# Shorter filler matmuls in the attention steps of an eight-core attention and expert layer

## What is computed

```python
h = _layernorm(x) * (1 + ca) + sa
x = x + ga * attn(h)
h = _layernorm(x) * (1 + cb) + sb
x = x + gb * ffn(h)

def attn(x):                       # 8 x 2048 x 1024, 16 heads of 64
    Q, K, V = x @ wq + bq, x @ wk + bk, x @ wv + bv
    Q, K, V = (a.reshape(B * H, S, D) for a in (Q, K, V))
    attn = softmax(einsum('bqd,bkd->bqk', Q, K) / sqrt(D))
    ctx = einsum('bqk,bkd->bqd', attn, V).reshape(B, S, E)
    return _layernorm(ctx @ wo + bo + x)

def ffn(x):                        # 8 experts, a gate for each token
    weights = softmax(x @ gate_w + gate_b), those below 0.1 dropped, rescaled
    return sum(weights[:, e] * (x @ expert_w[e] + expert_b[e]) for e in range(8))
```

## Time and profile before

| | |
|---|---|
| median of 2 runs | 2497.0 us (2492.66 to 2501.34) |
| the profiled execution | 2490.43 us |
| its span, slowest core (7) | 2488.9 us; the cores from 2454.0 to 2488.9 |
| mean granted clock, core 7 | 0.841 (the cores from 0.839 to 0.847) |
| TensorE busy | 1823.1 us, 73% of the span |
| VectorE busy | 903.3 us, 36% |
| ScalarE busy | 720.5 us, 29% |

### The profile page before, as it was taken

How to read it: one execution, slowest core, us unless ns; L and a number is a source line. 1 busy time by engine, 2 the same in 40 slices (tenths; PEclk the granted TensorE clock), 3 DMA queues, 4 the chain that set the end, 5 groups by cost and what they waited for, 6 DMA issues and landing times.

```text
span 2488.9 us, 23765 instructions; the slowest of 8 cores (2454.0 to 2488.9 us)
## 1 busy us (share of the span) xinstructions
PE 1823.1 (73%) x7658; PEld 719.0 (29%) x7658; DVE 903.3 (36%) x1481; ACT 720.5 (29%) x692; POOL 42.6 (2%) x78
## 2 busy tenths in 40 slices
PE   0122069978958968877886995896888299999993
PEld 0000032232223224223223322422422134444441
DVE  1443050062163144335316215324432643333336
ACT  0000007607604622740660561373274000000000
POOL 0000000000000000000000000000000000000000
PEclk9855578889869879987897986997898589999997
DMA  8642940040022022013002102202200121232103
GB/s 224 192 125 41 221 152 1 1 148 1 1 73 76 1 72 77 1 53 97 1 28 83 39 1 72 76 1 72 77 1 5 21 47 34 35 54 48 34 1 135
DMA packets 41837, 150.48 MB, mean 60 GB/s; under 512 B 15597, under 2 KB 15597, under 8 KB 37112
## 3 DMA queue, kind: packets, MB, share of 16 engines
q0 software_dynamic: 20480, 96.51, 14.7%
q1 hardware_dynamic: 21240, 52.46, 6.9%
HBM read 151.09 MB, written 16.78 MB: 67 GB/s over the span
## 4 chain that ended last, share of the span: by engine, by line
PE 56%; DVE 11%; ACT 8%; issue 5%; DMA 4%; DVEq 2%; ACTq 1%; POOLq 0%; SPq 0%
PE pbA L1083 9%; PE pbB L1083 9%; PE pbC L868 9%; PE pbD L914 6%; PE pbA L895 5%; ACT hT L906 5%; PE pbB L895 5%; DMA wbuf<-wbh 3%; PE pbA L771 3%; PE pbD L920 2%; PE pbD L616 2%; PE pbD L743 2%; DVEq L54 2%; DVE recipB L951 2%; ACT recipB L936 1%
## 5 line engine op out<-in xcount | busy, mean ns | idle before, releaser
L906 ACT ACTIVATE hT<-pbA,cm,c 128x1024 bf16<-128x1024 f32 x256 | 308.6, 1206 | 477.0 <-PE pbA L895 473.0
L868 PE MATMUL pbC<-hT,Vbuf 128*65 128x512 bf16 x1024 | 336.4, 413 | 40.8 <-ACT hT L906 38.1
L906 ACT ACTIVATE hT<-pbB,cm,c 128x1024 bf16<-128x1024 f32 x256 | 308.7, 1206 | 96.8 <-PE pbB L895 91.5
L951 DVE CAST recipB<-pbD 64x1024 bf16<-64x1024 f32 x32 | 38.9, 1217 | 797.7 <-PE pbD L946 797.7
L1083 PE MATMUL pbA<-We,h2T 128*128 128x512 bf16 x1024 | 232.8, 381 | 1.8 <-DVE facc L1056 1.8
L1083 PE MATMUL pbB<-We,h2T 128*128 128x512 bf16 x1024 | 231.5, 379 | 0.0
L914 PE MATMUL pbD<-CAb 128*128 128x512 bf16 x512 | 213.9, 418 | 22.4 <-DVE recipB L951 22.4
L895 PE MATMUL pbA<-Qasm,Kasm 64*128 64x512 bf16 x512 | 167.3, 409 | 1.1 <-DMA Kasm<-Kasm 1.1
L895 PE MATMUL pbB<-Qasm,Kasm 64*128 64x512 bf16 x512 | 166.3, 407 | 0.0
L771 PE MATMUL pbA<-hT,wbuf 128*128 128x256 bf16 x1024 | 145.1, 293 | 20.6 <-DVE Qasm L786 7.1
L920 PE MATMUL pbD<-CAb 128*128 128x256 bf16 x512 | 149.0, 291 | 0.0
(11 more groups left out here) (165 smaller groups left out, 1461.2 us busy)
## 6 DMA issues: line engine op xcount, KB each, us to landing
wbuf<-wbh POOLq DMA_DIRECT2D x32, 2048.0 KB, 9.4
wmstage<-wmod SPq DMA_DIRECT2D x32, 768.0 KB, 5.0
We<-ew POOLq DMA_DIRECT2D x8, 2048.0 KB, 14.5
xsb<-x SPq DMA_DIRECT2D x16, 512.0 KB, 14.4
wbh<-wbuf SPq DMA_DIRECT2D x4, 2048.0 KB, 12.9
out<-xsb SPq DMA_DIRECT2D x16, 512.0 KB, 2.7
wbuf<-wq POOLq DMA_DIRECT2D x1, 2048.0 KB, 18.6
wbuf<-wk POOLq DMA_DIRECT2D x1, 2048.0 KB, 38.4
```

What stands on the lines that cost most here:

```text
L868: P.emit("tensor", lambda e, h01=h01, gp=gp, q4=q4, par=par: e.matmul(psc[:, 512 * q4:512 * (q4 + 1)], vview[:, h01, gp, 0:65], PT[:, 1024 ...
L906: P.emit("scalar", lambda e, par=par: e.activation(PT[:, 1024 * par:1024 * (par + 1)], pss[par][:, :], AF.Exp, bias=cm3[:, :], scale=c0125 ...
L951: P.emit("vector", lambda e: e.tensor_copy(recipB[0:64, :], psr[:, :]), waits=[("t2", tv)], writes=("recipB",), inc="v1")
```

## The change

In every attention step the first filler shrinks from 512 columns to 128, and the second filler, 256 columns behind the context, goes. The increment of semaphore `m1` at step 15 moves to the filler that stays.

```diff
                     P.emit("tensor", lambda e: e.matmul(
-                        pbD[:, 0:512], CAb[:, 0:128], CAb[:, 0:512],
-                        start=True, stop=True), waits=fw)
+                        pbD[:, 0:128], CAb[:, 0:128], CAb[:, 0:128],
+                        start=True, stop=True), waits=fw,
+                        inc=("m1" if gp == 15 else None))
                     if pend is not None:
                         emit_mm2(*pend)
                     pend = (k, seg)
-                    P.emit("tensor", lambda e: e.matmul(
-                        pbD[:, 0:256], CAb[:, 0:128], CAb[:, 0:256],
-                        start=True, stop=True),
-                        inc=("m1" if gp == 15 else None))
```

## The result

| | before | changed |
|---|---|---|
| median | 2493.9 us (10 runs) | 2677.6 us (11 runs, lowest 2661.6) |
| ratio | 1 | 1.0716, 95% interval 1.0686 to 1.0747 |
| span of the slowest core, profiled | 2488.9 us | 2666.2 us (core 0) |
| mean granted clock of that core | 0.841 | 0.711 |
| first segments of octets 1 to 7 at full clock, all cores | 55 of 56 | 47 of 56 |

Some executions of a program on eight cores run with one die's clock held lower whatever the kernel; they are in the medians of this text but in none of its ratios or profiles, and where they leave only one or two others (runs 8, 9 and 12), the times of these stand in place of a median and a ratio.

What follows compares the result with a forecast made beforehand. The prediction took TensorE to pace the attention steps, with the granted clock deciding. Its terms (+151 later segments, +29 boundaries, +8 and -8 first segments, -23 luck) sum to +157, about 2647, stated as 2650 us, range 2550 to 2730.

Steps and rivals of the forecast that it cites:

- 24 later segments, luck included: Attention segments after each octet's first: 32.7 us each at half clock against 26.4, +151 us, before savings from lucky ones.
- their boundaries: Stretches between segments' exponentials, 4.5 us before: reached at half clock, each takes +1.2 us, times 24, +29 us.
- eight first segments: First segment of each octet: octet 0's stays at half clock, +8 us; seven at full clock save 1.2 us each, -8.
- outside attention: Projections, out-projection and experts: nothing moves, as they wait on transfers or run dense.
- The 23 us of luck: Later segments on core 7: 2 of 24 keep full clock, each 11.7 us better than a slow one, -23 us.
- The pace is TensorE's at half clock: Half-clock attention step: TensorE stays the pace, 2.08 us a step against 2.57, bounds 2.01 to 2.12.
- A segment that has fallen doesn't come back: Later segments: without fillers using the array both ways, half clock lasts through the 16 steps; 32.7 us; chance 0.55.
- The boundary takes the clock, the fillers ahead of the broadcast lift it first: Between segments: eight fillers, 3.4 us at half clock, lift the clock; broadcast, 64-row scores and two waits drop it again.
- A full-clock step of 1.32 us: Full-clock attention step: the loop through TensorE and ScalarE sets 1.32 us instead of 1.39, saving 1.2 us a segment.
- First segments stay at full clock: Octets' seven later first segments, behind the V projection and sixteen full fillers: they keep full clock, 22.2 us each.
- the fourth rival: Octets' first segments: full clock is lost there too, seven more at 32.7 instead of 22.2 us, +73: 2720; chance 0.12.
- The rule on idle gaps: Attention steps: if only long idle gaps cost clock, shorter segments stay at full clock, 22.2 us: 2380 us; chance 0.06.

Runs made afterwards that it cites:

- run 8: Changed kernel with 11 instead of 8 fillers at each segment's end, the waits behind the broadcast left empty; 2521.0 us in one execution.
- run 9: Changed kernel with boundary waits filled, no drain ahead of exponentials, and the start of first segments filled too; 2384.3 and 2394.1 us in two executions.
- run 12: Kernel before with all filler columns and rows, but filler weights of 64 instead of 128 columns; 2807.6 us in one execution.
- run 1: Kernel before with both step fillers reading 64 instead of 128 rows, columns unchanged; 2829.2 us, ratio 1.134.
- run 5: Kernel before, step fillers untouched, with extra fillers in the boundary's waits (11 at the end, 4 behind first scores, 1 ahead of first context pair); 2426.3 us, ratio 0.972.
- run 6: Changed kernel with extra fillers in the boundary's waits (11 at the end, 4 behind first scores, 3 ahead of first context pair); 2475.5 us, ratio 0.992.
- run 4: Changed kernel without the drain that ScalarE executes ahead of each exponential; 2659.5 us, ratio 1.065.
- run 2: Kernel before with only the second step filler (256 columns) removed, the 512-column one kept; 2523.1 us, ratio 1.010.
- run 3: Changed kernel with its 128-column step filler deleted too, the eight fillers at each segment's end kept; 2663.5 us, ratio 1.067.

## Why the prediction was right, and where it was off

The forecast was 2650 us in a range of 2550 to 2730 and slower; measured were 2677.6. Term by term, core 0's span is 177.3 us above core 7's before (2666.2 - 2488.9):

| term | forecast | measured |
|---|---|---|
| 24 later segments, luck included | +151 - 21 | +128 (761.6 - 633.2) |
| their boundaries | +29 - 2 | +22 (132.3 - 109.9) |
| eight first segments | 8 - 8 = 0 | +21 (210.1 - 189.2) |
| outside attention | 0 | +6 |
| sum | +157 | +177 |

(The 23 us of luck are split here as 21 in the segments and 2 in the boundaries. The boundaries are the times between one segment's last exponential and the next one's first.)

- **The pace is TensorE's at half clock.** Right. 2.04 us a step against 2.08 forecast; the filler of 128 columns costs 0.08 there, not 0.13. A half-clock segment is 32.2 us, forecast 32.7.
- **A segment that has fallen doesn't come back.** Right: 0 of 183 came back. Its reason is right too as far as rows go: run 1 changed only the rows that the fillers read, and 0 of 180 came back. That it must be the full array both ways was argued and is not shown (run 12).
- **The boundary takes the clock, the fillers ahead of the broadcast lift it first.** Right: the timeline above shows both, and runs 5 and 6 turn it round by filling the waits. That three more fillers ahead of the broadcast would be enough in most boundaries was not foreseen (run 8).
- **Luck: 2 of 24.** 19 of 192, or 2.4 of 24, over all cores; 1 on core 0.
- **A full-clock step of 1.32 us.** Wrong, and this is the step of the prediction that failed: "exponential k+1 starts and runs 1.21", with ScalarE's floor set at 1.21. The floor is 1.39. The 0.19 us of idle time in the earlier trace rows was put down to scores in the profile before, but a drain ahead of every exponential costs as much; the two ends came at the same moment. Run 4 took the drain away and found 21.7 us a segment where the forecast had 22.2. It cost the sum 8 us on its seven first segments (+8.4 not saved).
- **First segments stay at full clock.** Mostly right, 47 of 56, but wrong on the slowest core, where three of eight are at half clock (that of octet 0 was forecast). That is the rest of the +21: the fourth rival, realised in part. The forecast said nothing of the first steps' waits. The one for the first exponential is 0.69 us where it was 0.27, since long fillers had stood in it. The one for K's copy is there in both kernels, but not in every octet: all nine first segments that fell had it, 0.85 us on average, and only 11 of the 47 that held (over 0.1 us, all cores). Run 9 filled both and all 56 held.
- **The rule on idle gaps** of the Trainium skill ("TensorE: Matmul & The Clock Gate", section "Why this matters for your kernels"), which made the change a gain, did not carry here: no wait of TensorE in a boundary of the changed kernel is longer than 0.94 us, and filling them is worth about 200 us there (run 6), and 70 us in the kernel before (run 5).
- **Two of the signs.** The mean clock fell further than the 0.75 forecast, to 0.71. And line 868's waits for the exponential, which were to multiply, did not (waits of TensorE on core 0; 54 times and 38.1 us in the earlier trace rows):

```profile
PE pbC L868 <- ACT hT L906: 30.0, 50, 2.0
```

The net error on the span is 20 us: 21 in the first segments (8 of savings that were not there, 15 of two at half clock that were not foreseen, less 2 on the first octet's) and 6 outside attention, less 2 in the later segments and 5 in their boundaries.

Three numbers in the prediction are wrong in themselves. The fillers of a step before were 768 of 2816 columns (27%), not 640, which is what the change takes away; the text of run 2 repeats it as 23%. Twelve of the 24 later segments have a mean clock of 0.87, not thirteen. The likeliest case's upper end adds up to 2686 us (2650 + 14 + 22), not 2695. No term of the sum uses any of them.

## What to carry to other kernels

Price a filler matmul by what it buys, not by its columns: here each half-clock segment of 16 steps lasts 32 us and each at full clock 23, and trimming inside the half-clock step does not make up for that: 2.57 to 2.04 us a step leaves 32 us, and with no filler at all (1.96 us, run 3) a later segment still takes 30.6. Find the waits that cost the clock and put the fillers there, before shortening those in the steady part; only then does the next bound, here a drain of 0.19 us ahead of each exponential, show up as time. Look for waits inside the steady part too: with short fillers the clock fell behind the steps in which four small activations held TensorE up (run 6). When two engines' bounds are of the same height, a profile names only the one that came last, so test the other before counting on a gain below it.

## What the runs showed of the hardware

- With the same columns and the same steps, fillers reading 64 instead of 128 rows left 12 instead of 83 of 192 later segments at full clock, and the clock came back in 0 of 180 segments instead of 160 of 160 (run 1).
- The same short-filler steps kept full clock from the first to the last exponential in 150 of 192 segments (run 6) but never got back to it from half clock (0 of 183, the changed kernel).
- Dense fillers at the end of a segment brought the clock up, and 3.6 us with two score pairs and little else brought it down again (timeline of the changed kernel), though not in most boundaries when eleven fillers stood ahead instead of eight (run 8).
- With a drain ahead of each, exponentials of 1.20 us whose scores were ready started 1.39 us apart; without it, as little as 1.13 us (run 4). A segment at full clock went from 23.2 to 21.7 us.
- A filler with weights of 64 columns made the following context pair start 0.16 us later at half clock than one with 128 (0.56 against 0.40 us, run 12).
